# A two-layer sequence model on eight cores: eight expert halves instead of ten beside the scan

## What is computed

```python
def step(state, inp):                       # the scan, 2048 steps in series
    u_t, sp_t = inp
    state = jnp.tanh(state @ A.T + u_t @ B.T) + sp_t
    y_t = state @ C.T
    return (state, y_t)
...
# the experts: E = 8, hidden 4096, all computed for every token,
# weighted by a gate that is zero but for the two largest
h = jax.nn.relu(jnp.einsum('nd,edh->neh', x_flat, w1) + b1)
y = jnp.einsum('neh,eho->neo', h, w2) + b2
out_flat = jnp.einsum('ne,neo->no', dense_gate, y)
```

## Time and profile before

| | us |
|---|---|
| median of 2 runs | 8556.56 |
| lowest and highest | 8546.47 and 8566.64 |
| profiled execution, time | 8563.41 |
| profiled execution, span of the slowest core (core 5) | 8562.0 |
| spans of the eight cores | 8540.8 to 8562.0 |

### The profile page before, as it was taken

The page is one execution under the profiler, slowest core; times in us unless marked ns, Lnnn a source line. Parts: engine busy times, 40 slices in busy tenths (PEclk is TensorE's granted clock), DMA queues, the critical chain, the costliest instruction groups (busy, mean ns, idle before and its releaser), DMA issues.

```text
span 8562.0 us, 83520 instructions; the slowest of 8 cores (8540.8 to 8562.0 us)
## 1 busy us (share of the span) xinstructions
PE 6019.1 (70%) x24427; PEld 2378.4 (28%) x24427; DVE 2787.9 (33%) x4296; ACT 1546.4 (18%) x3342; POOL 358.4 (4%) x556
## 2 busy tenths in 40 slices
PE   2258888874988888988888988835456555655545
PEld 1112222222433333433333434311112111211121
DVE  0011111113222222322222222255554555455554
ACT  2323333320101001001010010102112211221111
POOL 0000010000000000000000000000000000000010
PEclk6556566565999999999999999965556555655677
DMA  1034343420122221133222223110000000000012
GB/s 45 0 51 73 57 74 58 62 53 13 28 40 40 40 40 30 26 49 50 45 40 40 40 42 49 28 13 3 10 10 8 3 10 10 6 5 5 0 19 51
DMA packets 157524, 271.38 MB, mean 32 GB/s; under 512 B 65158, under 2 KB 65718, under 8 KB 155062
## 3 DMA queue, kind: packets, MB, share of 16 engines
q0 software_dynamic: 146816, 234.00, 18.1%
q1 hardware_dynamic: 10294, 32.04, 1.3%
HBM read 483.05 MB, written 8.39 MB: 57 GB/s over the span
## 4 chain that ended last, share of the span: by engine, by line
PE 54%; DMA 16%; DVE 16%; issue 8%; ACT 5%; DVEq 1%; ACTq 0%; POOLq 0%; SPq 0%; PEldq 0%
PE psA L1029 47%; DMA w1b<-w 9%; PE psB L1029 7%; DVE mcols L1029 4%; DMA w2c<-w 3%; DMA w1f<-w 3%; ACT tanh_bf L1029 2%; ACT PT L1029 2%; DVE xA L1029 2%; DVE Qpair L1029 1%; DVE qraw L1029 1%; DVE mtmp L1029 1%; DVE rowT L1029 1%; DVE mcol L1029 1%; ACT rowT L1029 1%
## 5 line engine op out<-in xcount | busy, mean ns | idle before, releaser
L1029 PE MATMUL psA<-xS,w1b 128*128 128x512 bf16 x7552 | 1906.1, 402 | 345.3 <-DMA w1b<-w 339.5
L1029 PE MATMUL psA<-hbuf,w2c 128*128 128x512 bf16 x8192 | 1820.4, 385 | 65.7 <-DVE hbuf L1029 65.7
L1029 DVE TENSOR_SCALAR hbuf<-psA,b1c 128x512 bf16<-128x512 f32 x512 | 384.4, 751 | 2481.2 <-PE psA L1029 2481.2
L1029 PEld LDWEIGHTS psA<-hbuf,w2c 128*128 128x128 bf16 x8192 | 800.9, 99 | 1064.5 <-issue 179.7
L1029 PEld LDWEIGHTS psA<-xS,w1b 128*128 128x128 bf16 x7552 | 747.2, 99 | 1195.6 <-issue 407.6
L1029 ACT ACTIVATE tanh_bf<-psB,c_n 128x1 bf16<-128x1 f32 x2047 | 539.1, 263 | 1066.4 <-PE psB L1029 1066.4
L1029 PE MATMUL psB<-tanh_bf,AT_s 128*128 128x1 bf16 x2047 | 334.8, 164 | 438.3 <-ACT tanh_bf L1029 369.0
L1029 ACT ACTIVATE hbuf<-psA,b1c 128x512 bf16<-128x512 f32 x512 | 351.9, 687 | 1386.1 <-PE psA L1029 1374.8
L1029 PEld LDWEIGHTS psB<-tanh_bf,AT_s 128*128 128x128 bf16 x2047 | 212.6, 104 | 1081.6 <-issue 1075.4
L1029 ACT ACTIVATE PT<-psA 128x512 bf16<-128x512 f32 (+3 forms) x448 | 308.6, 689 | 1023.4 <-PE psA L1029 1011.5
L1029 DVE SCALAR_TENSOR_TENSOR ytmp<-psA,b2c,g_sb 128x512 f32<-128x512 f32 x256 | 192.2, 751 | 575.8 <-PE psA L1029 575.8
(11 more groups left out here) (155 smaller groups left out, 3836.6 us busy)
## 6 DMA issues: line engine op xcount, KB each, us to landing
w2c<-w POOLq DMA_DIRECT2D x208, 512.0 KB, 5.4
w1b<-w POOLq DMA_DIRECT2D x168, 512.0 KB, 5.3
w1f<-w POOLq DMA_DIRECT2D x80, 256.0 KB, 4.2
xA<-xT SPq DMA_DIRECT2D x8, 1024.0 KB, 17.3
out<-ost SPq DMA_DIRECT2D x8, 1024.0 KB, 12.2
xA<-xT SPq DMA_DIRECT2D x8, 768.0 KB, 15.2
Qh<-Qpair SPq DMA_DIRECT2D x16, 256.0 KB, 3.4
Kh<-Qpair SPq DMA_DIRECT2D x16, 256.0 KB, 3.4
```

The costliest lines, as they stand in the source:

```text
L1029: ins = getattr(eng_obj, method)(*args, **kw)
```

## The change

One constant goes from 10 to 8.

```diff
@@ -310,7 +310,7 @@
           AF.Tanh, bias=cbias, w=(("spe", t),), s="act", chain=False)
 
     CH_NTS = ((0,), (1, 2, 3))
-    KA = 10
+    KA = 8
     mark("P2_scan")
     for t in range(0, TS):
         scan_step(t)
```

## The result

| | before | after |
|---|---|---|
| runs | 42 | 43 |
| median, us | 8664.31 | 8698.57 |
| lowest to highest, us | 8542.57 to 9100.84 | 8607.91 to 9215.94 |
| profiled execution: span, us | 8562.0 | 8615.1 |

In a part of the executions of either kernel one die or both are granted a lower clock and the time rises by up to some 7%, so the medians over all runs say little, the ratios are taken from undisturbed runs alone, and where a profiled execution is disturbed on one die, a core of the other die is read and named. The ratio is 1.0067, with a 95% interval of 1.0042 to 1.0093. The change makes the kernel slower by 0.7%, +57 us on the median of 8556.6 that stood ahead of the prediction. The profiled executions differ by 53.1 us.

The account below looks back on a forecast made before the run. The scan's serial chain was taken to bound first products beside the scan, matmuls the second products. The scan stage gives -62 us, mix and c1 +114, so +52: 8615 us profiled, 8609 us against the median of 8556.6; range 8580 to 8650 us.

Parts of the forecast that it names:

- the dear clock: Second products beside the scan at a granted clock of about 0.79, 34.5 to 38.0 us each; all eight there: +26 us.
- first products beside the scan: Scan stage, first products: 1455 steps at 0.67 us whatever the halves, 1008.80 to 1002 us, a gain of 7 us.
- second products beside the scan: Scan stage, second products: two of ten windows of 33.0 us leave, -66 us, doubled steps add 11, net -55 us.
- mix and c1: Stages after the scan: tile 0 of two halves is added, two passes of 57.1 us, +114 us.
- layer 1: Layer 1: holds no work that KA touches, unchanged at about 3019 us.
- the joints: First products beside the scan: start of a half and steps held up behind an evacuation on ScalarE, 3.4 us a half.
- doubled steps: Second products beside the scan: 17 times a second step is emitted in a hook, 0.67 us each, +11 us.
- The pass: Mix and c1: one tile of a half through both products, 57.1 us, bounds 55.5 and 63 us.
- Nothing comes back: Rival, scan stage: it gives back nothing, only the +114 us remain, 8671 us, +1.3%; chance 0.04.
- matmul bound: Rival, scan stage: matmuls bound it, two of ten halves leave, -268 us, 8403 us, -1.8%; chance 0.03.
- low clock: Rival, second products beside the scan: TensorE stays at 1.2 GHz, +174 us, 8783 us, +2.6%; chance 0.02.
- The dear clock spreads: Rival: all eight second products at 36.3 us and moved matmuls at 0.27 us, 8662 us, +1.2%; chance 0.08.

Follow-up runs that it names:

- the run with KA = 16: KA = 16 against the kernel before, steps spread over both products and weight transfers not waiting for each other; span 7795.1 us.

## Why the prediction was right or wrong

**The time was outside the range.** The forecast was 8609 us in 8580 to 8650, the median came out at 8698.57. The step that failed is the last line of the sum, "against the median of 8556.6", and the 10 us that the range took in "for the spread of the runs shown". Two runs, 20 us apart, stood for the kernel before. Over 42 runs its own median is 8664.31, 108 us higher, with runs up to 9100.84. The range of a time has to hold the level of the base as well as the effect, and two close runs are no measure of the level. The profile of one execution doesn't give that spread either. The effect itself was forecast at +0.6% and measured at +0.67% (0.42 to 0.93), and the profiled execution was forecast at 8615 us and shows a span of 8615.1. That the last figure fits to a microsecond is luck: the terms below miss in both directions, and the 53 us between the two profiled cores hold a clock that the change has nothing to do with. The last column compares cores without the dear clock: six of the kernel before and all eight after, in the median.

| term | forecast, us | profiled cores, us | cores alike, us |
|---|---|---|---|
| first products beside the scan | -7 | -12.0 | -13 |
| second products beside the scan | -55 | -59.8 | -43 |
| mix and c1 | +114 | about +123 | +119 |
| layer 1 | 0 | about +1 | -1 |

**First products.** The mechanism held. A step costs 0.67 us with one matmul beside it or none, and taking half of the matmuls away changed a first product by 0.2 us. The size was off by 5 us: the joints are 2.7 us a half ((996.77 - 975)/8), not 3.4.

**Second products.** Eight were forecast at 33.0 us, the mean of the old ones, plus 11 us for doubled steps, 275 in all; the eight measured sum to 270.2. Two errors nearly cancel here. The 33.0 us had the dear clock in it: 31.1 is the mean on core 3, so the base was 16 us too high. The doubled steps were put at 0.67 us each, 11 us in all, and cost about 20: the term left out what TensorE waits for beside the tanh before its matmuls go on. The clock, called the widest unknown, took the cheap side: all eight windows lie at 0.91 to 0.95, none at 0.79. "I see nothing that ties it to KA" was right, and the other cores of the same trace could have shown it, since six of eight ran the same products at 0.90 or more. Why cores 4 and 5 alone stood at 0.79 stays open. The prediction took these windows to agree with the rule of the Trainium skill (TensorE: Matmul & The Clock Gate, The HAM clock gate) that a whole die goes to 13/16; cores 6 and 7, of the same die, stood at 0.90 and above in the same products, so the figure fits and the extent doesn't.

**Mix and c1.** The pass came out at 57.3 us (249.2 a half over four tiles, (5422.86 - 4079.55)/7 = 191.9 over three), for 57.1 forecast. The other 8 us are halves of the same kind that were 0.5 to 0.7 us longer than before, 16 times over. The waits for w1b hold 5 of them: they sum to 255.7 us over 15 halves, where before the same view had 294.0 us over 16 with the first load's 43.2 in it, so 250.8. The rest is within what the cores of one execution differ by, 6 to 10 us over the mix and c1. One reading of rows was wrong. I took 18.20 and 14.52 us in the earlier trace rows as waits behind four tiles and three. In both kernels they alternate from half to half instead: 18.79 and 16.27 us open the second and third half of the mix after the change, 20.77 and 16.08 the second and third of c1, and 14.25 us stood at the start of c1 before, behind four tiles. The shorter one is the half that starts an expert, and there TensorE first waits some 3 us for the gate row (`brow_g`: 21.3 us, 7 times, over the mix and c1). The conclusion, that the number of tiles doesn't set it, was right by another route.

The rows for that, changed kernel, timeline of TensorE:

```profile
2335.71 1.86 PE L1029 MATMUL psA<-xS,w1b 128*128 128x512 bf16 x4 [18.79 <-DMA w1b<-w]
...
2585.87 0.59 PE L1029 MATMUL psA<-xS,w1b 128*128 128x512 bf16 x1 [16.27 <-DMA w1b<-w]
...
4274.16 1.44 PE L1029 MATMUL psA<-xS,w1b 128*128 128x512 bf16 x3 [20.77 <-DMA w1b<-w]
...
4467.25 1.01 PE L1029 MATMUL psA<-xS,w1b 128*128 128x512 bf16 x2 [16.08 <-DMA w1b<-w]
```

**The rivals.** "Nothing comes back" is out by the 72 us of the stage (56 on cores without the dear clock), "matmul bound" and "low clock" by the run with half of the matmuls. "The dear clock spreads" didn't come: the second products stood at 0.91 and above, and the mix at 0.96, as before.

## What to carry to other kernels

Where a serial chain runs beside matmuls, ask of each stretch which of the two ends last, and price a unit of work by the stretch it leaves and the one it enters: here a pass was worth 28 us beside the scan (36 on the profiled cores) and about 60 in the mix, and the sign of the change followed. Before a mean over windows goes into a sum, look at the same windows on other cores: the profiled core owed some 18 us to a clock that six others didn't have. Then put the links of the chain where the matmuls are dense: spreading the same 1536 steps over both products was worth 171 us, three times the effect of the change, and only then did the transfers show as the next bound. A forecast of a time needs the spread of the base over many runs; a forecast of a ratio doesn't.

## What the runs showed of the hardware

- A step of the chain, TensorE product to ScalarE tanh and back, costs 0.67 us with no or one 128x512 matmul between at the lower clock level, and 0.83 us with two. At the upper level (granted 1.00, KA = 10, steps spread) it costs 0.67 us with two as well.
- Two steps in a row inside a dense stream of matmuls hold the stream up for 1.15 us, a single one for 0.03 us.
- Two cores of a die can be granted a lower clock than their neighbours in the same execution: in the kernel before, cores 4 and 5 stood at 0.78 to 0.80 in four second products (37.5 us where core 3 took 33.1), and in the run with KA = 16 cores 6 and 7 at 0.81 for some 400 us.
- A high busy share in the profile doesn't tell a high clock. In the first products before, TensorE is shown busy for 82 of 100 us at a granted clock of 0.50 to 0.53 of 2.4 GHz, at or near the lower level (1.2 GHz). Over the stage with the steps spread at KA = 10 it is shown busy for 865 of 1112 us, a smaller share, at 0.97, near the upper one.
- Eight transfers of 512 KB in turn kept TensorE waiting for 43.5 us, eight under way together for 27.8 us.
- Behind a wait of 18.79 us for weights the granted clock was 0.50 for the next 5 us, and 128 matmuls took 30.46 us and not 27.79.
